# A sorted mixture of experts: the first product with its weights standing still, and routed weights copied to a fixed place

## What is computed

```
# l2f, x normalized to xf [2048, 256]; 8 experts, hidden 512, top 2
shared_out = (silu(xf @ sw1) * (xf @ sw3)) @ sw2
rw, sel    = top_k(xf @ router_w + experts_bias, 2);  rw = softmax(rw)
eo_e       = silu(xf @ w1_e) * (xf @ w3_e)
x          = x + shared_out + sum_e cw_e * (eo_e @ w2_e)
# l3f: the shared expert alike (hidden 512); routed experts hidden 256, one first product:
y_e        = gelu(xf @ ew1_e) @ ew2_e
```

## Time and profile before

| what | us |
|---|---|
| median of 3 runs (3393.85 to 3400.02) | 3397.52 |
| the profiled execution, its own time | 3404.03 |
| its span, first to last instruction | 3402.2 |
| busy in the span: PE | 3212.0 (94%) |
| PEld (overlaps PE) | 2578.8 (76%) |
| DVE | 2261.8 (66%) |
| ACT | 1460.8 (43%) |
| POOL | 1051.6 (31%) |

### The profile page before, as it was taken

The page is one execution under the profiler, slowest core; times in us unless marked ns, Lnnn a source line. Parts: engine busy times, 40 slices in busy tenths (PEclk is TensorE's granted clock), DMA queues, the critical chain, the costliest instruction groups (busy, mean ns, idle before and its releaser), DMA issues. The chain is left out here.

```text
span 3402.2 us, 105709 instructions
## 1 busy us (share of the span) xinstructions
PE 3212.0 (94%) x39150; PEld 2578.8 (76%) x39150; DVE 2261.8 (66%) x7473; ACT 1460.8 (43%) x4214; POOL 1051.6 (31%) x1684
## 2 busy tenths in 40 slices
PE   8979899999997999999999999889999999998899
PEld 6758787788776888888778778776666787877676
DVE  3766325777757888888847777775334577777655
ACT  2335335666633333333336656552111455555432
POOL 0114112333343444444523333344111111114441
PEclk8999899999988999999999999898999999999799
DMA  5654331112202000000011111006111111110333
GB/s 205 211 180 173 114 113 60 59 56 71 66 32 116 2 2 2 2 2 2 2 43 42 49 45 59 2 17 241 47 45 68 36 40 40 43 42 2 99 104 113
DMA packets 145873, 225.27 MB, mean 66 GB/s; under 512 B 14216, under 2 KB 121480, under 8 KB 143816
## 3 DMA queue, kind: packets, MB, share of 16 engines
q1 hardware_dynamic: 138816, 203.16, 18.5%
q0 software_dynamic: 6816, 18.69, 1.5%
HBM read 201.03 MB, written 38.74 MB: 70 GB/s over the span
## 5 line engine op out<-in xcount | busy, mean ns | idle before, releaser
L3398 POOL TENSOR_TENSOR l1fu_second_weighed<-l1fu_second,l1fu_parts 128x256 bf16<-128x256 bf16 x384 | 275.2, 744 | 339.0 <-DVE l1fu_second L3646 335.6
L3450 PEld LDWEIGHTS l1fu_ps_u<-l1f_xnT_all,l1f_key_in 128*128 128x128 f32 x2048 | 249.8, 193 | 7.7 <-issue 1.5
L3450 PE MATMUL l1fu_ps_u<-l1f_xnT_all,l1f_key_in 128*128 (+1 forms) x2048 | 251.4, 277 | 0.0
L3519 ACT COPY l1fu_plane<-l1fu_ps_p 128x512 f32<-128x512 f32 x128 | 74.9, 585 | 260.8 <-PE l1fu_ps_p L3440 260.8
L3641 DVE TENSOR_TENSOR l1fu_first<-l1fu_index,l1fu_counted 128x1024 bf16<-128x1024 bf16 x128 | 165.2, 1291 | 17.3 <-PE l1fu_ps_p L3440 15.1
L3461 PE MATMUL l1fu_ps_y<-l1f_key_out,l1fu_units_rest 128*128 128x256 f32 x704 | 171.5, 388 | 1.6 <-DVE l1fu_units_rest L3654 1.6
L3461 PEld LDWEIGHTS l1fu_ps_y<-l1f_key_out,l1fu_units_rest 128*128 128x128 f32 x704 | 127.7, 190 | 21.9 <-issue 2.9
L3440 PE MATMUL l1fu_ps_p<-l1fu_second_weighed,l1fu_first 64*128 64x32 bf16 x6144 | 114.5, 192 | 22.9 <-POOL l1fu_second_weighed L3398 14.9
L1073 ACT ACTIVATE l1x_scores<-l1x_scores,l1x_minus_big 128x257 f32<-128x257 f32 x256 | 129.1, 516 | 12.0 <-DVE l1x_minus_big L1159 10.4
L1073 ACT ACTIVATE l2x_scores<-l2x_scores,l2x_minus_big 128x257 f32<-128x257 f32 x256 | 129.1, 516 | 12.0 <-DVE l2x_minus_big L1159 10.4
L1073 ACT ACTIVATE l3x_scores<-l3x_scores,l3x_minus_big 128x257 f32<-128x257 f32 x256 | 128.6, 505 | 10.8 <-DVE l3x_minus_big L1159 9.7
(11 more groups left out here) (759 smaller groups left out, 8653.1 us busy)
## 6 DMA issues: line engine op xcount, KB each, us to landing
rows_by_expert<-in_zeros_dram SPq DMA_DIRECT2D x1, 17544.0 KB
l0x_ctxT<-in_ctx_T_dram SPq DMA_DIRECT2D x32, 514.0 KB, 5.1
l0x_ctx_rows<-in_ctx_dram SPq DMA_DIRECT2D x64, 256.0 KB, 3.3
l0f_w<-in_L_ffn_w_dram SPq DMA_DIRECT2D x16, 1024.0 KB, 5.1
l1x_ctx_sb<-in_ctx_T_dram SPq DMA_DIRECT2D x60, 256.0 KB, 3.2
l2x_ctx_sb<-in_ctx_T_dram SPq DMA_DIRECT2D x60, 256.0 KB, 3.0
l3x_ctx_sb<-in_ctx_T_dram SPq DMA_DIRECT2D x60, 256.0 KB, 2.7
l1x_mask_raw<-in_mask_int_dram SPq DMA_DIRECT2D x16, 514.0 KB, 4.2
```

The lines of the kernel that those rows point to most:

```text
L3398: last = nc.gpsimd.tensor_tensor(second_weighed[:, k % 2, part], second[:, k % 2], parts[:, 1 - par, part, TC * k:TC * k + TC].unsqueeze(2 ...
L3450: last = nc.tensor.matmul(ps_u[:, k % 2, j, :], key_in[:, c, JS * k + j, :], xnT_all[:, c, bass.ts(tile, P)], start=(c == 0), stop=(c == C ...
L3519: nc.scalar.copy(plane[:, par].rearrange("p j (h n) -> p h j n", h=2)[:, :, :, TC * k:TC * k + TC], ps_p).then_inc(s["plane_kept"], 1)
```

## The change

The first product is done the other way round: `up` lets a 128x128 piece of the weights stand and moves the 128 columns of `xsT`. The result comes out with hidden units on the partitions, which is the form that `down` needs, so `turn_hidden`, `keep_hiddenT`, `ps_h` and `hiddenT` go. `activate` and `gate_hidden` work on the same number of elements as before. PE's turn n becomes `turn_rows(n + 1)`, `up(n)`, `down(n - 1)`; only the first routed block's rows (n + 1 = FIRST) are still turned after `up(n)`. `keep_rowsT` runs two blocks ahead of `activate`.

A routed block's weights no longer stand at an address worked out on PE: they are copied to `placed_up` beforehand. In l2f DVE copies 1024 elements per partition for the gate half and 1024 for the up half of each block (`place_half`), into a single buffer; in l3f ACT copies 512 per block (`place_gates`), into two. Each engine loads the block's expert number for that itself.

```diff
-            def up(n, at):
+            def up(n):
                 w = weights_of(n)
+                b = order[n][1]
+                weights = placed_up[:, b % halves] if is_routed(n) else ws.up[:, 0]
...
                 for a, dst in enumerate((ps_g, ps_u)[:w.ups]):
-                    for c in range(C):
-                        last = nc.tensor.matmul(dst[:, 0:w.hidden], xsT[:, n % 2, c, :],
-                                                w.up[:, at, a, c, :].rearrange("p e n -> p (e n)"),
-                                                start=(c == 0), stop=(c == C - 1))
+                    if is_routed(n):
+                        pe.wait_ge(s["gates_placed" if a == 0 else "ups_placed"], b + 1)
+                    for hc in range(w.hidden // P):
+                        units = slice(hc * P, hc * P + P)
+                        for c in range(C):
+                            last = nc.tensor.matmul(dst[:, units], weights[:, a, c, units], xsT[:, n % 2, c, :],
+                                                    start=(c == 0), stop=(c == C - 1))
...
-            def turn_hidden(n):
...
             def down(n, at):
-                pe.wait_ge(s["hiddenT_ready"], n + 1)
+                pe.wait_ge(s["hidden_ready"], n + 1)
                 after(pe, s["y_ready"], n)
...
             for n in range(N):
+                if n + 1 < N and n + 1 != FIRST:
+                    turn_rows(n + 1)
                 at[n] = expert_of_block(n)
-                up(n, at[n])
+                up(n)
+                if n + 1 == FIRST:
+                    turn_rows(n + 1)
                 if n:
-                    turn_hidden(n - 1)
-                if n + 1 < N:
-                    turn_rows(n + 1)
-                if n > 1:
-                    down(n - 2, at[n - 2])
+                    down(n - 1, at[n - 1])
...
-            turn_hidden(N - 1)
-            down(N - 2, at[N - 2])
             down(N - 1, at[N - 1])
...
+            def place_gates(b):
...
+                after(act, s["gate_up_ready"], FIRST + b - 1 if b > 1 else 0)
+                at = bass.ds(act.value_load(expert_i[0:1, b:b + 1], min_val=0, max_val=E - 1), 1)
+                nc.scalar.copy(placed_up[:, b % 2, 0].rearrange("p c n -> p (c n)"),
+                               wr.up[:, at, 0].rearrange("p e c n -> p (e c n)")).then_inc(s["gates_placed"], 1)
             keep_rowsT(0)
+            keep_rowsT(1)
             for n in range(N):
                 activate(n)
-                if n + 1 < N:
-                    keep_rowsT(n + 1)
+                if not wr.swiglu and 0 <= n + 2 - FIRST < RB:
+                    place_gates(n + 2 - FIRST)
+                if n + 2 < N:
+                    keep_rowsT(n + 2)
...
+            def place_half(b, a):
+                at = bass.ds(dve.value_load(expert_i[0:1, b:b + 1], min_val=0, max_val=E - 1), 1) if a == 0 else placing
+                nc.vector.tensor_copy(placed_up[:, 0, a].rearrange("p c n -> p (c n)"),
+                                      wr.up[:, at, a].rearrange("p e c n -> p (e c n)")).then_inc(
+                                          s["gates_placed" if a == 0 else "ups_placed"], 1)
...
             for n in range(N):
+                placing_next = wr.swiglu and 0 <= n + 1 - FIRST < RB
+                if placing_next:
+                    b = n + 1 - FIRST
...
+                        dve.wait_ge(s["gate_up_ready"], n + 1)
+                    placing = place_half(b, 0)
                 gate_hidden(n)
+                if placing_next:
+                    if b:
+                        dve.wait_ge(s["up_ready"], swiglu_blocks(n + 1))
+                    place_half(b, 1)
                 if is_routed(n):
                     name_home(order[n][1])
                 if n:
-                    keep_hiddenT(n - 1)
-                if n > 1:
-                    keep_y(n - 2, merged_by(n))
+                    keep_y(n - 1, merged_by(n))
```

More of the change, by code:

```diff
@@ L2645, in sorted_experts_ffn @@
             chosen_ready ranked positions_ready experts_ready blocks_ready dump_ready scattered
-            turned xsT_ready gate_up_ready up_ready activated hidden_ready hidden_turned hiddenT_ready
+            turned xsT_ready gate_up_ready up_ready activated gates_placed ups_placed hidden_ready
             down_ready y_ready home_named home_ready first_added combined x_stored""")
@@ L2664, in sorted_experts_ffn @@
         xsT = sb("xsT", [P, 2, C, P])
-        hidden = sb("hidden", [P, 2, HMAX])
-        hiddenT = sb("hiddenT", [P, 2, HMAX // P, P])
+        hidden = sb("hidden", [P, 2, HMAX // P, P])
+        halves = 1 if wr.swiglu else 2
+        placed_up = sb("placed_up", [P, halves, wr.ups, C, wr.hidden])
         y = sb("y", [P, RING, D])
@@ L2695, in sorted_experts_ffn @@
         ps_x, ps_g, ps_u = ps("ps_x", [P, 2, 512]), ps("ps_g", [P, 512]), ps("ps_u", [P, 512])
-        ps_h, ps_d, ps_r = ps("ps_h", [P, 512]), ps("ps_d", [P, 512]), ps("ps_r", [P, 512])
+        ps_d, ps_r = ps("ps_d", [P, 512]), ps("ps_r", [P, 512])
         ps_l = core.pair_bank if core.number + 1 in core.context_loaded else ps("ps_l", [P, 512])
@@ L2866, in down @@
                 HC = w.hidden // P
-                pe.wait_ge(s["hiddenT_ready"], n + 1)
+                pe.wait_ge(s["hidden_ready"], n + 1)
                 after(pe, s["y_ready"], n)
                 for hc in range(HC):
-                    last = nc.tensor.matmul(ps_d[:, 0:D], hiddenT[:, n % 2, hc, :],
+                    last = nc.tensor.matmul(ps_d[:, 0:D], hidden[:, n % 2, hc, :],
                                             w.down[:, at, hc, :].rearrange("p e n -> p (e n)"),
@@ L2929, in activate @@
                 act.wait_ge(s["gate_up_ready"], n + 1)
-                after(act, s["hidden_turned"], n - 1)
-                rows = hidden[:, n % 2, 0:w.hidden]
+                after(act, s["down_ready"], n - 1)
+                rows = hidden[:, n % 2].rearrange("p h n -> p (h n)")[:, 0:w.hidden]
                 if w.swiglu:
@@ L3108, in gate_hidden @@
                     dve.wait_ge(s["up_ready"], swiglu_blocks(n + 1))
[L3109 to L3117, removed]
+                    units = hidden[:, n % 2].rearrange("p h n -> p (h n)")[:, 0:w.hidden]
+                    nc.vector.tensor_tensor(units, units, ps_u[:, 0:w.hidden], ALU.mult).then_inc(s["hidden_ready"], 1)
             def keep_y(n, merged):
@@ L3130, in combine @@
             def combine(i, n):
-                dve.wait_ge(s["y_ready"], n - 1)
+                dve.wait_ge(s["y_ready"], n)
                 dve.wait_ge(y_loaded[i // GT], 16)
@@ L3178, in _ @@
                     combine(i, n)
-            keep_hiddenT(N - 1)
-            keep_y(N - 2, NT)
             keep_y(N - 1, NT)
```

13 lines of the change are left out of this document (8 added, 5 removed).

## The result

| what | before | after |
|---|---|---|
| median of 5 runs, us | 3393.85 (3388.64 to 3400.02) | 3361.11 (3354.75 to 3371.70) |
| ratio, 95% interval | | 0.9903 [0.9878, 0.9927] |
| profiled execution, own time / span, us | 3404.03 / 3402.2 | 3355.71 / 3353.8 |

The change makes the kernel faster by 32.7 us, where 28 were forecast. Two more runs of before came with the result, so its median is 3393.85 and not the 3397.52 that the forecast started from.

The account below looks back on a forecast made before the run. PE's columns were taken to bound both loops: 28.5 us gained there, +0.5 for the edges, so -28 from 3397.5 gives 3369.5 us. Its own range was 3364 to 3374; 3361 to 3382 was given to hold 8 in 10.

Parts of the forecast that it names:

- the term for the two ends of each loop: Opening and end of l2f's and l3f's loops: waits saved and added, together 0 to +1 us, taken as +0.5.
- The new first product: `up` on PE: 128-column matmuls 0.111 to 0.112 us apart, dearer by 0.12 to 0.15 us per 512-unit block.
- Rival 2: `up` on PE: weight loads of 0.190 us set the pace without overlapping each other, +174 us, 3572; 4 in 100.
- The transposes and the columns' sum: PE in both loops: transposes of hidden go, less the dearer first product, 27.3 to 29.8 us gained, taken as 28.5.
- The base: Starting time of the forecast: median of before 3397.5 us, or 3404.0 for the profiled execution, each less 28.
- Placing on DVE: l2f: two copies a block of 0.69 to 1.29 us each, upper end taken; DVE's turn at worst 5.2 of 5.52, costing PE nothing.
- Placing on ACT: l3f: a copy of 0.37 to 0.61 us plus register load a block; ACT's sum 1.3 to 1.87 of 1.98, taken as hidden.
- tightest margin: ACT in l3f: sum of 1.3 to 1.87 us against a period of 1.98, and 2.05 with the longest register load.
- Turning the rows earlier: `turn_rows` ahead of `up`: sorted rows wanted earlier; SP issues loads about 6 us ahead, 3.1 us bounds the first, so it holds.
- 1 (ACT's pace): l3f: ACT's block of 2.25 us exceeds PE's 1.98, giving back 10.5 us, 3380; 8 in 100.
- 3 (DVE's pace): l2f: dearer copies and hops; each 0.1 us over 5.52 costs 3.9 us, all 28 gone at 6.24; 6 in 100.
- 4 (the opening set by POOL's scatter): Each sublayer's opening: savings of the first seven blocks are waited away at the first sorted rows, 4 us back, 3373.5; 5 in 100.

Follow-up runs that it names:

- rows after: Changed kernel with all rows turned after the first product and ACT copying them one block ahead, behind the placing copy; one run, 3394.70 us.

## Why the mechanism was right, and which term of the sum failed

**The step that failed** is the term for the two ends of each loop. It was put at +0.5 us, with bounds of 0 to +1, and it measured -2.9. The loops gained 31.3 us, outside the 27 to 30 that the forecast allowed. The new first product, the transposes and both placings came out as forecast; what was wrong in the sum, besides its base, was this term, and it is taken apart below.

**What bounds the loops** was read rightly: PE's work, which fills both of them. Both periods came out as forecast, 5.52 and 1.98.

**The new first product** is 0.1116 per matmul in runs of 32, between the 0.111 and 0.112 taken from runs of 16. Rival 2 falls: in the 210 us of l2f's blocks lie 1600 loads of about 0.19 us, which would be 304 us one after another, so they overlap each other. Priced at 0.190 a matmul, the rival had the loops grow by 174 us, and they shrank by 31. This is where the Trainium skill's rule (TensorE: Matmul & The Clock Gate, Part 3, The mechanism), by which a load overlaps matmuls in flight only when it targets other rows of the array, differs from the measurement, and the measurement decides. The same section of the Trainium skill also lets PE pull ahead a load that targets the background weight buffer, and no run here shows whether that is what these loads do. The 174 is the price of loads that don't overlap each other; loads that waited for the matmuls too would cost more.

**The transposes and the columns' sum:** 55 x 0.296 = 16.3 and 39 x 0.188 + 16 x 0.296 = 12.1, together 28.4, where I took 28.5.

**The ends, the term that was mis-sized:** 31.3 - 28.4 says -2.9 in place of +0.5. The bounds of 0 to +1 didn't follow from their own parts either, which add to +0.2 to +1.0. By rows, start to start: PE's wait for the ranks is gone, -0.95 in l3f and -0.49 in l2f, because the shorter pipeline brings a second product ahead of it; this I hadn't seen, having looked only at the wait for the table chain, which grew by less than 0.1 in place of 0.2. The end of the loop gave -0.41 twice, where 0 to -0.2 was allowed. One pair of transposes in each opening now runs while PE waits for ACT anyway, -0.22 twice. The clock's moment gave -0.9 in l3f and took 0.7 in l2f, as it fell in this execution. And the cost that I did put in, 0.2 to 0.4 for the seventh block's gelu behind `keep_rowsT(7)`, isn't there. PE's rows of after's timeline from the first sorted rows to the first routed product show no idle time:

```profile
2339.77 0.38 PE L2830 MATMUL l2f_ps_x<-const,l2f_xs 128*128 128x128 f32 x2
2339.99 1.89 PE L2868 MATMUL l2f_ps_d<-l2fs_w_down,l2f_hidden 128*128 128x256 f32 x8
2341.72 0.38 PE L2830 MATMUL l2f_ps_x<-const,l2f_xs 128*128 128x128 f32 x2
2341.94 1.97 PE L2858 MATMUL l2f_ps_g<-l2f_xsT,l2f_placed_up 128*128 128x128 f32 x16
```
Together these parts are -2.8. The old lag, put back in l3f alone, made its loop 3.0 longer, 2.5 without the first product. That confirms in kind the ranks' wait and the end's, which in l3f are 0.95 and 0.41 by the rows of before and after; in the kernel with the old lag both waits are longer than they were in before.

**The base** was the other part of the 8.4 us between 3369.5 and 3361.1. The forecast stood on a median of three runs, 3397.52; five gave 3393.85, and the later sets of 11, 11 and 17 runs gave 3394.91, 3395.35 and 3397.65. So this part is spread and no step of the working. On the base of 3393.85 the same sum gives 3365.9, and the columns' term with the ends as measured 3362.5, against 3361.1. The base's share of the error (3.7) is as large as that of the ends (3.4). From the profiled execution the sum gave 3376.0, and after's was 3355.7: 20.3 us off, of which 17 lie in the untouched sublayers.

**Placing on DVE** is hidden, and the copy costs 0.69, the lower bound and not the 1.29 that I chose: I took the row with the same count of elements, and the one with the same type and half the count came out equal; no run here shows why. It did no harm, as the order had been worked through with the upper end. DVE's turn is 0.69 x 3 + 0.42 + 2 x 0.21 = 2.9 of 5.52.

**Placing on ACT** is hidden. 0.62 is 0.01 over the upper bound. The "tightest margin" was far wider: a second copy fits, a third doesn't. The register load, which I added to ACT's turn at 0.30 to 0.49, shows as 0.24 idle where ACT has time, 0.14 with two copies and nothing with three.

**Turning the rows earlier** was priced as a moved 0.22 us and looked at for what it asks of SP and POOL. Its main effect was missed: it gives ACT's copy of rows a block's time, so that the placing copy may stand ahead of it. Without it, in the given order on ACT, l3f's loop is 30 us longer and all but 1.7 of the 31.3 us are gone (rows after). That l3f's period came out as forecast is luck in this respect: the change has the order that it needs, and nothing in the forecast's working says so.

**Rivals.** 1 (ACT's pace) and 3 (DVE's pace): not here, but reached with two further copies on ACT and with three further ones per half on DVE. 2: refuted above. 4 (the opening set by POOL's scatter): the first sorted rows, turned at 2339.77, made no wait. Loads have become the next wait, though, once the opening is shortened by more.

**Open** is what makes the untouched sublayers take 2870 to 2887 us from execution to execution. No experiment was made on that. Of the 18 us up to l2x, before and after differ by 9 in the first three sublayers (516 against 507 us), by 4 in the 100 us from 948 on, where the granted clock was 0.88 in before and 0.93 in after, and by 4 in the 680 behind them (0.98 against 0.99).

## What to carry to other kernels

Where a matmul's result must be transposed to be the next one's standing operand, turn the first product round instead: the columns are the same, and the price is only that of more and shorter instructions, so measure their spacing in the longest run that the change makes. Before a copy is put on a second engine, don't sum that engine's turn, but ask which of its instructions the bounding engine waits for next and put the copy behind it, or give that instruction a block more of time. Price a loop's change by its period times the blocks, then go through its opening and its end wait by wait, the waits that may vanish as well as those that may grow, and compare loops and not spans when the rest of the program varies by half of what is sought.

## What the runs showed of the hardware that I had not expected

- Runs of 32 float32 matmuls with 128 moving columns, each with a 128x128 load of 192 ns of its own, follow each other at 111.6 ns, and PE has no gap in 210 us of such blocks.
- A float32 copy of 128x1024 in SBUF takes DVE 0.69 us, as long as an operation of two operands on 128x512, one of them in PSUM.
- The register load ahead of a copy shows as 0.24 to 0.25 us of idle time on ACT in after, as 0.14 with two copies, and as nothing with three.
- Durations of neighbouring instructions on a full ACT overlap: 2.61 us of them take 2.37.
